# Second layer's attention: key tiles taken in pairs, with one group of four 32-row products for the maxima of both

## What is computed

```
q_hk   = (hidden_q @ Wq.T).reshape(b, s, H, K)          # H = 16 heads, K = 128
q_big  = einsum('bshk,hkq->bshq', q_hk, w_kc_q)
q_r    = einsum('bshq,hqr->bhsr', q_big, W_qr)
k_r    = einsum('bld,hdr->bhlr', kv_rope, W_kr)
scores = einsum('bhsr,bhlr->bhsl', q_r, k_r)            # 16 x 56 queries, 1500 keys
attn   = softmax(scores, axis=-1)
ctx_c  = einsum('bhsl,bld->bhsd', attn, kv_rope)        # 64 channels
out    = (ctx_c with w_kc_kv, then Wo)
```

## Time and profile before

| what | us |
|---|---|
| runs: median of three (lowest, highest) | 3187.75 (3183.57, 3194.1) |
| the profiled execution | 3174.48 |
| its span | 3172.7 |
| granted clock of TensorE, mean over the span | 0.957 |

### The profile page before, as it was taken

One profiled execution on the slowest core, in us unless ns is written; L12 is line 12 of the kernel. 1 busy time (PEld: TensorE's weight loads), 2 busy tenths in 40 slices (PEclk: granted clock), 3 DMA queues, 4 the chain that ended last, 5 costly groups with the idle time before them and its releaser, 6 DMA issues. The chain is left out here.

```text
span 3172.7 us, 42691 instructions
## 1 busy us (share of the span) xinstructions
PE 2859.5 (90%) x15992; PEld 1636.7 (52%) x15992; DVE 1959.1 (62%) x2330; ACT 1181.8 (37%) x1648; POOL 1668.2 (53%) x935
## 2 busy tenths in 40 slices
PE   7689999989999999996899979999999999986998
PEld 6544445444544454443788844444454454435665
DVE  3386667676766686754666466655655655636664
ACT  3124441445144423442333234444443443433331
POOL 0267766767667775772200047677676666741111
PEclk9689999999999999998999989999999999997999
DMA  8233331334123322322000043332223232300000
GB/s 288 86 92 80 80 103 34 80 80 105 45 66 83 94 67 55 80 52 88 1 1 1 21 90 79 72 73 68 69 70 72 66 74 64 83 29 25 6 6 12
DMA packets 98869, 209.17 MB, mean 66 GB/s; under 512 B 30306, under 2 KB 74322, under 8 KB 91116
## 3 DMA queue, kind: packets, MB, share of 16 engines
q1 hardware_dynamic: 98668, 206.44, 25.0%
HBM read 135.36 MB, written 46.00 MB: 57 GB/s over the span
## 5 line engine op out<-in xcount | busy, mean ns | idle before, releaser
L1129 POOL TENSOR_TENSOR sums<-sums,prob 125x896 f32<-125x896 f32 x556 | 1177.1, 2117 | 282.5 <-ACT prob L1069 239.5
L1216 DVE TENSOR_REDUCE maxpart<-pair 112x2 f32<-112x1000 f32 x744 | 889.5, 1196 | 449.5 <-PE pair L931 448.9
L1069 ACT ACTIVATE prob<-wide 125x896 f32<-125x896 f32 x768 | 704.4, 917 | 902.9 <-PE wide L957 898.9
L971 PE MATMUL single<-prob,kv 125*64 125x448 f32 x3072 | 753.6, 569 | 0.5
L952 PE MATMUL wide<-qhigh,kparts 64*125 64x448 f32 x3072 | 448.8, 369 | 1.5 <-DVE maxpart L1216 1.5
L931 PE MATMUL pair<-kparts,qhigh 64*112 64x500 f32 x1488 | 360.9, 481 | 86.1 <-DVE maxpart L1216 84.7
L931 PEld LDWEIGHTS pair<-kparts,qhigh 64*112 64x112 f32 x1488 | 130.2, 172 | 517.9 <-DVE maxpart L1216 438.6
L1129 POOL TENSOR_TENSOR sums<-prob 125x896 f32<-125x896 f32 x64 | 134.7, 2104 | 362.3 <-ACT prob L1069 362.3
L952 PEld LDWEIGHTS wide<-qhigh,kparts 64*125 64x125 f32 x3072 | 281.7, 184 | 79.7 <-issue 48.2
L957 PE MATMUL wide<-shift,ones_row 64*125 64x448 f32 x1536 | 284.8, 365 | 5.1 <-DMA shift<-maxrow 5.0
L952 PE MATMUL wide<-qlow,kparts 64*125 64x448 f32 x1536 | 283.3, 363 | 0.0
(11 more groups left out here) (329 smaller groups left out, 3919.9 us busy)
## 6 DMA issues: line engine op xcount, KB each, us to landing
kparts<-keys_merged SPq DMA_DIRECT2D x64, 750.0 KB, 8.9
kparts<-kparts SPq DMA_DIRECT2D x96, 250.0 KB, 3.1
keys_merged<-kparts SPq DMA_DIRECT2D x32, 750.0 KB, 7.3
recip<-zrec_merged SPq DMA_DIRECT2D x124, 112.0 KB, 2.8
w_low_values<-w_merged SPq DMA_DIRECT2D x64, 192.0 KB, 2.4
raw<-in_ctx SPq DMA_DIRECT2D x32, 375.0 KB
values_merged<-kv SPq DMA_DIRECT2D x32, 375.0 KB
kv<-values_merged SPq DMA_DIRECT2D x32, 375.0 KB
```

The source lines that it names most:

```text
L971: mm = pe.matmul(mix_acc[64 * half:64 * half + DC, 0:HQ], kv[:, b % 3, t, :], prob[:, (b * LT + t) % NPROB, half * HQ:(half + 1) * HQ], st ...
L1069: nc.scalar.activation(prob[:, n_ % NPROB, :].rearrange("p (a b) -> p a b", a=2), acc[0:LP, :, 0:HQ], ACT.Exp)\
L1129: nc.gpsimd.tensor_tensor(dst, first_in, prob[:, n_ % NPROB, :], ALU.add).then_inc(s["pool_sum"], 1)
L1216: V.tensor_reduce(maxpart[:, b % 2, t:NMAX:4, third], acc[0:TQ, :, 0:LB], AX.X, ALU.max).then_inc(*R.signal_drained(kind, *key))
```

## The change

In the second layer the loop over 12 tiles becomes a loop over six pairs p. In a pair the six products of tile t go to region 0 and the six of tile t + 1 to region 1, and a new step `shift` then adds the maxima to both: four products of 32 rows each, of which the first two (rows 32 to 63 and 96 to 127) finish tile t, the other two (rows 0 to 31 and 64 to 95) tile t + 1. For that `ones_row` is 1 and `shift` holds the maxima in rows 0, 32, 64 and 96, so four DMAs fill `shift` for a batch where two did. The two `mix` steps of the pair before follow one another. The order of the steps that come once in a batch is rewritten: `fetch` and `norm` are at pair 1, `maxneg`, `maxT` and `spread` at pair 4, `share` at pair 5; at pair 4 `spread` now follows `maxT`. The first layer keeps its order of steps.

```
     for b in range(NB):
         g, j = divmod(b, BG)
-        for t in range(LT):
+        for p in range(LT // 2):
+            t = 2 * p
+            if p == 1 and b + 2 < NB:
                 add("fetch", b + 2)
-            add("score", b, t, region=t % 2)
-            if b + 1 < NB and t == 8:
+            ahead(b, t)
+            add("score", b, t, region=0)
+            add("score", b, t + 1, region=1)
+            add("shift", b, t)
+            if b + 1 < NB and p == 4:
                 add("maxneg", b + 1)
...
+            ahead(b, t + 1)
+            queries = g + 1 < G and j == BG - 2 and p < NPAIR // 2
+            if queries:
+                add("query", g + 1, t, region=3)
+            if p or b:
+                old = (b, t - 2) if p else (b - 1, LT - 2)
+                add("mix", old[0], old[1])
+                add("mix", old[0], old[1] + 1)
+                if not p:
                     add("context", b - 1)
-            if t == 1 and b:
+            if p == 1 and b:
                 add("norm", b - 1, region=3)
-            if b + 1 < NB and t == 9:
+            if b + 1 < NB and p == 4:
                 add("maxT", b + 1, region=3)
...
+            if queries:
+                add("query", g + 1, t + 1, region=3)
+            if g and j == 1 and 1 <= p <= 3:
+                for m, half in (((0, 0),), ((0, 1),), ((1, 0), (1, 1)))[p - 1]:
+                    add("project", g - 1, m, half, region=None if half else 3)
             if g + 1 < G and j == BG - 3:
-                if t == 2:
+                if p == 1:
                     add("mean", g + 1, region=3)
...
-                if t in (7, 8):
-                    add("rstd", g + 1, t - 7)
-                if t == 10:
+                if p >= 4:
+                    add("rstd", g + 1, p - 4)
+                if p == 5:
                     add("xsplit", g + 1)
...
-            if t == 8 and b:
+            if p == 4 and b:
                 add("spread", b - 1)
-            if t == 10 and b:
+            if p == 5 and b:
                 add("share", b - 1, 2)
...
-                    for half in range(2):
-                        sp.dma_start(shift[DC * half:DC * half + 1, b % 2, :].bitcast(F32),
-                                     maxrow[4 * half:4 * half + 4, b % 2, :].bitcast(F32)).then_inc(s["shift_loaded"], 16)
+                    for r in range(shift_copies):
+                        for half in range(2):
+                            sp.dma_start(shift[DC * half + 32 * r:DC * half + 32 * r + 1, b % 2, :].bitcast(F32),
+                                         maxrow[4 * half:4 * half + 4, b % 2, :].bitcast(F32)).then_inc(s["shift_loaded"], 16)
...
+                elif kind == "shift":
+                    b, t = key
                     if t == 0:
-                        pe.wait_ge(s["shift_loaded"], 32 * (b + 1))
...
+                        pe.wait_ge(s["shift_loaded"], 64 * (b + 1))
+                    for i in range(2):
+                        for half in range(2):
+                            at = DC * half + 32 * (1 - i)
+                            mm = pe.matmul(region[i][0:LP, half, 0:HQ], c["ones_row"][at:at + 32, 0:LP], shift[at:at + 32, b % 2, :],
+                                           start=False, stop=True)
+                        mm.then_inc(*R.signal_filled("score", b, t + i))
```

More of the change, by code:

```diff
@@ L112, in rolling_schedule, with ahead @@
         maximum(1, i, (PAIR, 0)[i % 2])
+    def ahead(b, t):
+        n = t + EARLY_MAX
+        due = (b + 1, n) if n < LT else (b + 2, n - LT)
+        if due[0] < NB:
+            maximum(*due)
     for b in range(NB):
         g, j = divmod(b, BG)
-        for t in range(LT):
-            ahead = (b + 1, t + EARLY_MAX) if t + EARLY_MAX < LT else (b + 2, t + EARLY_MAX - LT)
-            if t == 2 and b + 2 < NB:
+        for p in range(LT // 2):
+            t = 2 * p
+            if p == 1 and b + 2 < NB:
@@ L118, in rolling_schedule @@
                 add("fetch", b + 2)
-            add("score", b, t, region=t % 2)
-            if b + 1 < NB and t == 8:
-                add("maxneg", b + 1)
[L122 to L125, removed]
+            ahead(b, t)
[3 more added lines that the diff above has]
+            if b + 1 < NB and p == 4:
+                add("maxneg", b + 1)
@@ L130, in rolling_schedule @@
                 add("maxT", b + 1, region=3)
-            if g and j == 1 and t in (2, 3, 5, 6):
-                m, half = divmod((2, 3, 5, 6).index(t), 2)
-                add("project", g - 1, m, half, region=None if half else 3)
+            if queries:
[3 more added lines that the diff above has]
+                    add("project", g - 1, m, half, region=None if half else 3)
@@ L134, in rolling_schedule @@
             if g + 1 < G and j == BG - 3:
-                if t == 2:
+                if p == 1:
                     add("mean", g + 1, region=3)
-                if t in (3, 4):
-                    add("square", g + 1, t - 3)
-                if t == 5:
+                if p == 2:
+                    for k in range(KT):
+                        add("square", g + 1, k)
+                if p == 3:
                     add("var", g + 1, region=3)
-                if t in (7, 8):
-                    add("rstd", g + 1, t - 7)
@@ L152, in rolling_schedule @@
                 add("share", b - 1, 2)
+    add("mix", NB - 1, LT - 2)
     add("mix", NB - 1, LT - 1)
@@ L565, in _ @@
                 dve.wait_ge(setup_sems["setup_const"], 2)
-                for r in (0, DC):
+                for r in range(0, 128, 32):
                     nc.vector.memset(ones_row[r:r + 1, :].bitcast(F32), 1.0)
@@ L745, in attention @@
     mix_acc = region[2]
+    shift_copies = (1, 2)[layer]
     steps = attention_schedule(layer)
@@ L953, in _ @@
                                       start=(i == 0), stop=False)
-                    if t == 0:
-                        pe.wait_ge(s["shift_loaded"], 32 * (b + 1))
[L956 to L959, removed]
+                    if layer == 0:
+                        if t == 0:
+                            pe.wait_ge(s["shift_loaded"], 32 * (b + 1))
+                        for half in range(2):
+                            mm = pe.matmul(acc[0:LP, half, 0:HQ], c["ones_row"][rows_of(half), 0:LP], shift[rows_of(half), b % 2, :],
+                                           start=False, stop=True)
+                        mm.then_inc(*R.signal_filled(kind, *key))
+                elif kind == "shift":
+                    b, t = key
+                    if t == 0:
+                        pe.wait_ge(s["shift_loaded"], 64 * (b + 1))
+                    for i in range(2):
+                        for half in range(2):
+                            at = DC * half + 32 * (1 - i)
+                            mm = pe.matmul(region[i][0:LP, half, 0:HQ], c["ones_row"][at:at + 32, 0:LP], shift[at:at + 32, b % 2, :],
+                                           start=False, stop=True)
+                        mm.then_inc(*R.signal_filled("score", b, t + i))
                 elif kind == "mix":
@@ L1054, in _ @@
                     if b >= 2:
-                        act.wait_ge(s["shift_loaded"], 32 * (b - 1))
+                        act.wait_ge(s["shift_loaded"], 32 * shift_copies * (b - 1))
                     nc.scalar.activation(maxrow[:, b % 2, :], acc[0:NMAX, 0:TQ], ACT.Copy).then_inc(*R.signal_drained(kind, *key))
```

## The result

The changed kernel takes 3305.34 us in the median (3289.77 to 3325.45, four runs) where the kernel before takes 3188.56: a ratio of 1.0369, with an interval of 1.0306 to 1.0432. The profiled execution is 3298.13, with a span of 3296.4; against 3174.48 that is 124 us.

The account below looks back on a forecast made before the run. TensorE's own stream was taken as the bound, busy 90% of the span. Stall 88, two other batches -2, clock 66, next group's input 4 and queries 6 made 162 us on 3188: 3350, range 3275 to 3410.

Parts of the forecast that it names:

- likeliest mechanism: SyncE's queue delays spread's store, so share, a reduction and then TensorE wait, and its clock falls; given 62%.
- The pair: TensorE's stream for two tiles: 4.11 us against 4.26 before, 0.9 us less in a batch, 29 over 32 batches.
- that without a change of form: Lower bound of a pair: no change between 64 and 32 rows, weights loaded ahead, 3.76 us.
- that of two and two: Upper bound of a pair: the four 32-row products run two and two, 0.20 us more, 4.31.
- The queue: SyncE's queue: the store stands behind maxrow's wait and four shift DMAs, so share starts 12.25 us after pair 4's first smax.
- The stall: TensorE idle 4.31 us at the next pair's second smax, 2.94 slower per batch net, 30 times: 88 us.
- The clock: TensorE falls to half clock after each of 30 stalls, 2.2 us each, 66 us; bounds 0 and 2.9 each.
- Queries: Batch 6: two queries in one pair with one region, VectorE's low part later; 0.5 in each of 12 pairs, 6 us.
- The sum: Whole kernel: 88 - 2 + 66 + 4 + 6 = 162 us slower, 3350 on the runs' scale.
- the transfers come in time: Rival at share: ready before 9.3 instead of 12.25, so the stream's gain shows; 3155 with no stall; 4%.
- 32-row groups need no drain: Rival on TensorE: the array takes 32-row groups in its stride; 101 us slower, 3289, or 3241 without clock fall; 15%.
- the four run two and two: Rival on TensorE: the four 32-row products do not run side by side; some 209 us slower, 3397; 10%.

Follow-up runs that it names:

- the version with 64-row products: The first experiment's kernel, but the maxima of both tiles added by four 64-row products in two slots, with two shift DMAs; 3138.21 us, 0.9866 of the kernel before.
- The first experiment: The changed kernel with only spread moved, from the end of pair 4 to right behind maxneg; 3152.43 us, 0.9907 of the kernel before.

## Why the prediction was right, and which terms were off

The forecast was slower, 3350 within 3275 to 3410; it came out slower, at 3305. Its likeliest mechanism is the one that the runs show.

- *The pair.* 4.11 was forecast. From the second `smax` at 1917.43 to the next at 1921.72 there are 4.29, less 0.29 for `maxT`: 4.00, and without `maxT` 4.09 (1911.30 to 1915.39 in the same trace). Four 32-row products start together (within 0.01), and from them to the next `smax` it is 0.40, as forecast. Of the bounds, that without a change of form (3.76) and that of two and two (4.31) are both out. The Trainium skill's rule (TensorEngine Tiling (Array Packing), Key Properties) that a change of tiling mode drains the array agrees with this, and the version with 64-row products shows the price: 4.10 against 3.93. So the group of four costs 0.17 a pair more than the two slots that it replaces; what the pairs win, they win by the two `mix` steps that follow one another.
- *The queue.* From the first `smax` of pair 4 (1915.39): second `smax` 2.04, forecast 2.04; `maxT` 4.00, forecast 4.06; end of `maxrow` 4.66, forecast 4.71; store 7.24, forecast 7.5; loads 8.73, forecast 8.9; `share` 12.28, forecast 12.25. The idle time at `share` is 4.24, forecast 4.1.
- *The stall, mis-sized.* Forecast 4.31, shown 3.66 (1929.46, where 1925.40 + 0.40 would have done). The term that was off is `share` itself: I took 1.40 from the earlier trace rows, it took 0.62. In 7 of the first 29 batches it took 1.35 to 2.55, and there TensorE was idle some 5.6 us. Over the stage the wait of the rows above rose by 126.7 - 24.9 = 102 us; the forecast had 30 x (4.31 - 0.47) = 115. The count of 30 was off too: the last batch has no `smax`, which leaves 29 stalls, and in three of these, behind the batch that makes the next group's input, `share` waits for VectorE's own work and not for `recip`. The first experiment has the same idle time of 3.5 us there, so the queue's order makes 26 stalls. I had left these three batches at the price of the others.
- *The clock, mis-sized.* Forecast 66 us, 2.2 in each of 30 batches. Half of 106.3 less half of 13.1 is 47. There were 27 falls, 18 of 3.4 us and 9 of 6.8, which is 2.0 each on the mean, so the price of a fall was nearly right. Too high was their number: three of the 27 stand behind the next group's input, where the first experiment has falls as well, and I had taken nothing off for those that the kernel before had.
- *Queries.* I gave them 6 us. In the first experiment, where `spread` is not late, a batch with queries takes 46 to 47 us against 42.5 to 43.2 before, but the batch ahead of it 30.0 instead of 33.3 to 34.4, so the two have to be taken together. They take 77.5, 77.3 and 76.2 us against 75.8, 76.7 and 77.6: 1 us more, where the pairs should have saved 5. That is some 6 us in all, as forecast; how it divides between queries and input is not shown.
- *The sum.* 102 + 47 - 29 + 6 = 126, where the two profiled executions are 124 apart. In the first experiment TensorE waits for reductions as long as before (23.7 and 24.9), so the 102 are the queue's order alone. Of the forecast 162, the stall was 13 and the clock 19 too much, both to the same side; no two errors cancelled.

The rivals that the transfers come in time, that 32-row groups need no drain, and that the four run two and two are all excluded by these rows. The clock stayed full behind 2 of the 29 stalls.

## What to carry to other kernels

Where engines walk through one written order, a step that is moved is moved on every queue: `spread` cost SyncE three issues and VectorE 0.19 us, but behind `maxT` its transfers started 5 us later than in the first experiment (7.24 against 1.95 after the pair's first `smax`), and a wait in the order of one engine held up the bound one. Price a moved DMA by what is ahead of it in its queue, issue times included (0.57 to 0.63 us each in the changed kernel, for 1.8 KB), not by its landing time alone. And packing products into smaller row groups pays only if the slots saved exceed the changes of form: here a pair took 4.10 us with one group of four 32-row products, and 3.93 with two slots of 64-row products in its place.

## What the runs showed of the hardware that I had not expected

`share` on VectorE and the additions on GpSimd exclude each other. In the timeline above `share` starts first and takes 0.62; the addition that starts 0.05 later takes 2.51 instead of some 2.1. In another batch, the addition was first:

```profile
2099.46 2.07 POOL L1156 TENSOR_TENSOR sums<-prob 125x896 f32<-125x896 f32 x1 [2.79 <-ACT prob L1096]
2100.24 1.77 DVE L1307 TENSOR_TENSOR ctx_n<-ctx_raw,recip 128x448 f32<-128x448 f32 x1 [5.06 <-DMA recip<-zrec_merged]
```

It ends at 2101.53, and `share` 0.48 behind it; so it is in all 8 batches in which an addition was running when `share` started, and for the squares of the 64-row version. The Trainium skill has this (SBUF — State Buffer, SBUF: two separate sides: the port pair that the two share goes to whichever starts first, for the whole instruction), and the trace agrees; I had read the 1.40 of the earlier trace rows as the operation's own time, where 0.62 is the operation and the rest was a wait. The reductions, which read PSUM, took 1.14 to 1.20 throughout the stage.
